# Attention followed by a mixture of experts: eight splits, two bias loads and the last adds moved between engines

## What is computed

```python
x = x + attention(layernorm(x), ctx)      # 4x1024 rows of 256, 16 heads of 64, 64 keys of 192
x = x + ffn(layernorm(x))

def ffn(x):                                # E = 8 experts, top 2, H = 352
    scores = softmax(x @ gate_w.T)
    idx = top_k(scores + gate_b, 2)
    h  = silu((x @ w1[e] + b1[e]) * (x @ w3[e] + b3[e]))     # for the two experts e of a row
    y  = sum over the two of scores[e] * (h @ w2[e] + b2[e])
    z  = the same form with the shared weights sw1, sw3, sw2 (every row)
    return y + z
```

## Time and profile before

| | |
|---|---|
| time, median of three runs | 722.57 us (722.37 to 724.9) |
| the profiled execution | 728.77 us, its span 727.0 us, mean granted clock 0.974 |
| busy: TensorE, VectorE, ScalarE, GpSimd | 92%, 74%, 55%, 59% of the span |
| attention's pipeline | about 95 to 335 us |
| units' phase | 339 to 725 us |

### The profile page before, as it was taken

One profiled execution on the slowest core, in us unless ns is written; L12 is line 12 of the kernel. 1 busy time (PEld: TensorE's weight loads), 2 busy tenths in 40 slices (PEclk: granted clock), 3 DMA queues, 4 the chain that ended last, 5 costly groups with the idle time before them and its releaser, 6 DMA issues.

```text
span 727.0 us, 16811 instructions
## 1 busy us (share of the span) xinstructions
PE 671.5 (92%) x4606; PEld 627.8 (86%) x4607; DVE 537.7 (74%) x1106; ACT 400.9 (55%) x1308; POOL 429.1 (59%) x514
## 2 busy tenths in 40 slices
PE   7997789999999989985699999999999999999976
PEld 6785679998888879874699999999999999999975
DVE  5964788888978878766989866666666666666796
ACT  4984677877767666664564444444444444444432
POOL 4552565454468677665346337677777777775291
PEclk8998999999999999996999999999999999999999
DMA  8201223336526875754851335554444444455694
GB/s 247 78 15 65 66 73 94 104 110 193 161 80 116 187 138 130 111 133 90 154 85 44 79 49 75 75 74 72 72 73 72 72 72 72 72 102 97 150 407 187
DMA packets 77045, 79.03 MB, mean 109 GB/s; under 512 B 21738, under 2 KB 70228, under 8 KB 76980
## 3 DMA queue, kind: packets, MB, share of 16 engines
q1 hardware_dynamic: 56932, 53.66, 29.3%
q0 software_dynamic: 15760, 18.96, 16.2%
q10 hardware_dynamic: 4288, 5.64, 2.4%
HBM read 47.22 MB, written 31.01 MB: 108 GB/s over the span
## 4 chain that ended last, share of the span: by engine, by line
PE 32%; issue 22%; POOL 13%; DMA 11%; SPq 9%; DVE 7%; ACT 5%; POOLq 0%; ACTq 0%; DVEq 0%
PE ps L1269 26%; DMA slots_scratch<-record,slot 8%; POOL xrow L718 6%; SPq L542 5%; SPq L543 4%; PE ps L1376 3%; POOL acc_scratch L725 2%; POOL slots_scratch L668 2%; DMA xin<-in_x 1%; PE ps L1360 1%; ACT prob L791 1%; DVE AU L1121 1%; DMA wk_raw<-in_L_xattn_Wk 1%; PE ps L1345 1%; ACT AU L803 1%
## 5 line engine op out<-in xcount | busy, mean ns | idle before, releaser
L725 POOL DMA_INDIRECT acc_scratch<-yrow,slots x71 | 112.7, 1587 | 70.2 <-ACT yrow L920 56.3
L920 ACT ACTIVATE yrow<-ps,slots 128x256 f32<-128x256 f32 x71 | 33.7, 474 | 147.7 <-PE ps L1269 147.7
L1269 PE MATMUL ps<-AU,pTh 128*128 128x256 f32 x512 | 101.3, 290 | 0.0
L1195 DVE TENSOR_TENSOR uv<-ps,b 128x704 f32<-128x704 f32 x71 | 63.3, 892 | 47.8 <-PE ps L1269 47.8
L1269 PE MATMUL ps<-w13h,uxTh 128*128 x284 | 97.8, 344 | 0.0
L1269 PE MATMUL ps<-AU,xTh 128*128 128x512 f32 x256 | 97.4, 425 | 0.0
L668 POOL DMA_INDIRECT slots_scratch<-record,slot x64 | 66.1, 1033 | 45.8 <-DMA slots_scratch<-record,slot 33.6
L1269 PE MATMUL ps<-w13h,uxTl 128*128 x284 | 91.6, 322 | 0.0
L1269 PE MATMUL ps<-w13l,uxTh 128*128 x284 | 91.3, 322 | 0.0
L718 POOL DMA_INDIRECT xrow<-xn_scratch,slots x71 | 69.8, 983 | 27.2 <-issue 19.8
L791 ACT ACTIVATE prob<-ps,nmax 128x64 f32<-128x64 f32 x256 | 76.3, 337 | 14.4 <-DVE nmax L1048 14.3
(11 more groups left out here) (241 smaller groups left out, 2000.9 us busy)
## 6 DMA issues: line engine op xcount, KB each, us to landing
sums<-acc_scratch SPq DMA_DIRECT2D x16, 512.0 KB, 11.3
w_raw<-in_L_ffn_w SPq DMA_DIRECT2D x16, 352.0 KB, 4.1
xin<-in_x SPq DMA_DIRECT2D x32, 128.0 KB, 2.5
xres<-in_x SPq DMA_DIRECT2D x32, 128.0 KB, 3.0
acc_scratch<-x SPq DMA_DIRECT2D x32, 128.0 KB, 2.3
xn_scratch<-xn SPq DMA_DIRECT2D x32, 128.0 KB, 2.6
xn2T_scratch<-xn2T SPq DMA_DIRECT2D x32, 128.0 KB, 3.7
xrow<-xn2T_scratch SPq DMA_DIRECT2D x32, 128.0 KB, 5.0
```

The source lines that it names most:

```text
L725: pool.indirect_dma_start(acc_dram[u % 2], bass.IndirectOffsetOnAxis(ap=slots[:, u, 0:1], axis=0), yrow[:, m % YRING, :], None, compute_op ...
L920: act.activation(yrow[:, y, :], ps[:, 6 + m % 2, 0:D], ACT.Copy, scale=slots[:, bass.ds(u, 1), 1].bitcast(F32)).then_inc(y_ok, 1)
L1195: dve.tensor_tensor(uv[:, :, :], ps[:, 1 + 2 * p:3 + 2 * p, 0:H], bias, ALU.add).then_inc(bias_ok, 1)
L1269: last = pe.matmul(out, stationary(k, a), moving(k, b), start=(k == 0 and i == 0), stop=(k == n - 1 and i == len(PARTS) - 1 and not more))
```

## The change

- The splits of the experts' first weights: `high13` of experts 0 to 4 at ScalarE's attention steps 30 to 34, `low13` of experts 0 to 4 at VectorE's attention steps 33 to 37; the remaining three low parts at steps 13 to 15 of the units' phase.
- The biases: a table [128, 2, 8, 352] is loaded with 2 transfers of 128 x 2816 values.
- Behind the routed units (t >= `R1`) ScalarE also copies the rows to PSUM, and VectorE's uxTl subtraction reads that copy; ScalarE waits for `uxTl_ok` of the last routed unit first.
- Quads 5, 6 and 7 are added by VectorE itself at steps 100, 101 and 102; the zrow adds of quads 5 and 6 stand at steps 101 and 103; VectorE no longer waits for GpSimd's adds.

```diff
-        b13 = sb("b13", [P, E, 2 * H], F32)
+        b13 = sb("b13", [P, 2, E, H], F32)
...
-            for e in range(E):
-                for i, b in enumerate((b1, b3)):
-                    sp.dma_start(b13[:, e, i * H:(i + 1) * H],
-                                 b[e, :].rearrange("(a h) -> a h", a=1).to_broadcast([P, H])).then_inc(b13_in, 16)
+            for i, b in enumerate((b1, b3)):
+                sp.dma_start(b13[:, i, :, :].rearrange("p e h -> p (e h)"),
+                             b.rearrange("(a e) h -> a (e h)", a=1).to_broadcast([P, E * H])).then_inc(b13_in, 16)
...
-            for q in range(NT // QUAD):
+            for q in range(NA // QUAD):
                 both = [sums[:, i, q, :, :].rearrange("p a d -> p (a d)") for i in range(2)]
                 pool.wait_ge(sums_in[q], 32)
                 pool.tensor_tensor(both[0], both[0], both[1], ALU.add).then_inc(both_ok, 1)
...
-                if 33 <= s < 33 + EARLY13:
-                    high13(s - 33)
+                if 30 <= s < 30 + EARLY13:
+                    high13(s - 30)
...
-                    act.activation(uxTh[:, p, :], xT, ACT.Copy).then_inc(uxTh_ok, 1)
+                    if isinstance(t, int) and t >= R1:
+                        act.wait_ge(uxTl_ok, R1)
+                        act.activation(uxTh[:, p, :], xT, ACT.Copy)
+                        act.activation(ps[:, 0, p * D:(p + 1) * D], xT, ACT.Copy).then_inc(uxTh_ok, 1)
+                    else:
+                        act.activation(uxTh[:, p, :], xT, ACT.Copy).then_inc(uxTh_ok, 1)
...
-                if s >= 35:
-                    low13(s - 35)
+                if 33 <= s < 33 + EARLY13:
+                    low13(s - 33)
...
-                    dve.wait_ge(both_ok, NT // QUAD)
...
-                    xT = ps[:, 0, 0:D] if is_routed(t, routed) else xrow[:, m, :]
+                    if is_routed(t, routed):
+                        xT = ps[:, 0, 0:D]
+                    elif t >= R1:
+                        xT = ps[:, 0, p * D:(p + 1) * D]
+                    else:
+                        xT = xrow[:, m, :]
...
-                if isinstance(s, int) and 5 + E <= s < 5 + E + E - 3:
-                    low13(s - 5 - E + 3)
-                q = s - NALL + NT // QUAD - 2 if isinstance(s, int) else -1
-                if NA // QUAD <= q < NT // QUAD - 1:
-                    z0 = (q - NA // QUAD) * QUAD
-                    row = sums[:, 0, q, :, :].rearrange("p a d -> p (a d)")
-                    dve.wait_ge(both_ok, q + 1)
+                if isinstance(s, int) and 5 + E <= s < 5 + E + E - EARLY13:
+                    low13(s - 5 - E + EARLY13)
+                if isinstance(s, int) and NALL - 3 <= s < NALL:
+                    q = s - NALL + NT // QUAD
+                    both = [sums[:, i, q, :, :].rearrange("p a d -> p (a d)") for i in range(2)]
+                    dve.wait_ge(sums_in[q], 32)
+                    link(dve.tensor_tensor(both[0], both[0], both[1], ALU.add))
+                if isinstance(s, int) and s in (NALL - 2, NALL):
+                    z0 = (s - NALL + 2) // 2 * QUAD
+                    row = sums[:, 0, (NA + z0) // QUAD, :, :].rearrange("p a d -> p (a d)")
                     dve.wait_ge(z_row_ok, z0 + QUAD)
```

More of the change, by code:

```diff
@@ L1188, in unit_step @@
                         if isinstance(t, int) and t == R0:
-                            dve.wait_ge(b13_in, 32 * E)
-                        bias = b13[:, bass.ds(e, 1), :].rearrange("p e (a h) -> p (e a) h", a=2)
+                            dve.wait_ge(b13_in, 32)
+                        bias = b13[:, :, bass.ds(e, 1), :].rearrange("p a e h -> p a (e h)")
                     else:
```

## The result

The changed kernel takes 729.86 us (median of 20 runs, 726.9 to 737.26). The kernel before, over its own 20 runs, takes 725.19 (722.37 to 729.03); its first three, from which the prediction started, gave 722.57. The ratio is 1.0066 [1.0048, 1.0084]: **4.8 us slower** (the medians are 4.7 apart), where +3.0 was forecast. The sign was right; the time lies 0.9 us above the range. Of the 4.3 us between 725.6 and 729.86, 2.6 are the starting figure, which three runs gave too low, and 1.7 are the change.

What follows compares the result with a forecast made beforehand. TensorE was taken as the bound, losing time in attention's last steps, the units' steps 13 to 17 and the tail. Attention +5.8, units -0.9, tail -1.9 gave +3.0 us: 725.6 us from 722.57, range 718.9 to 729.

Steps and rivals of the forecast that it cites:

- the clock: Attention's end: TensorE's clock falls in the pause ahead of ranks, the product behind mostly at half clock; +2.0 us (0 to +2.9).
- the copy: Behind the routed units: ScalarE's extra copy to PSUM is hidden, 0; without cover 4 us at most.
- the tail: Behind the routed units: fewer hold-ups of VectorE, partly eaten by its own three adds; -1.9 us (+1 to -5).
- ScalarE's three slots: Attention steps 30 to 32: high-part splits delay xn2T by +0.4, +0.95 and +1.35, in sum 2.7 us (0.4 to 4.1).
- The split of step 33: Attention step 33: VectorE's low part lies in its idle time; 0, without that cover 0.8 us.
- The split of step 34: Attention step 34: VectorE's low part directly ahead of the logits' copy delays ranks; +1.6 us (1.2 to 1.7).
- The units' phase: Routed units, steps 16 and 17: two splits fewer; -0.9 us (0 to -1.7).
- The sign that was to prove it wrong: Start of the units' phase, uxTl of tile 0 (before at 338.9), less than 2 us later.
- Rival 1: Attention's end: the clock holds, everything else as forecast without the 2.0; 723.6 us, chance 0.26.
- Rival 2: Drain's whole price: product wholly at half clock, step 33's split uncovered, tail gives only 0.9; +5.7, 728.3 us, chance 0.18.
- Rival 3: Whole tail comes back: step 99's product slips between GpSimd's adds, steps at 3.33 us; -5 there, 720.5 or 718, chance 0.17.
- Rival 4: Tail: lock by start order, VectorE's quads could hold up GpSimd's; no cost, or +1.5 with a late landing (727.1); chance 0.05.

Runs made afterwards that it cites:

- experiment 4: The changed kernel plus 20 unused identity transposes on TensorE in step 35, ahead of the wait for the ranks; 1.0023 of the kernel before.
- experiment 9: The kernel before with only the high parts moved to ScalarE's steps 30 to 34, low parts as before; 1.006 of the kernel before.
- a1: The kernel before with the new places of all the splits alone, high and low parts; 1.0056 of the kernel before.
- a3: The changed kernel without the split in step 34: VectorE's low parts at steps 33, 35, 36, 37, four in the units' phase; 1.0051 of the kernel before.
- b1: The changed kernel itself measured again, on another chip; 1.0067 of the kernel before.
- a4: The kernel of experiment 4: the changed kernel plus 20 unused transposes ahead of the wait for the ranks; 1.0023 of the kernel before.
- c3: The kernel of experiment 9: the kernel before with only ScalarE's high parts moved early; 1.006 of the kernel before.
- b2: The kernel before with only the biases loaded in two transfers; 0.9989 of the kernel before.
- b3: The kernel before with only VectorE's three quads: no PSUM copy, old bias loads and splits; 1.0018 of the kernel before.
- Experiments 7 and 8: 7: b3, and b4 with five copies (1.0018, 0.9995). 8: c4, the kernel before with 12 copies, GpSimd adding all quads (1.0002).
- a2: The changed kernel with the splits back at their places of before; 0.9955 of the kernel before.
- b4: The changed kernel with the splits of before and the PSUM copy in five steps instead of twelve; 0.9995 of the kernel before.
- c1: b4 plus unused transposes in the pauses of attention's steps 34 to 37 and ahead of the first unit; 0.9942 of the kernel before.
- c4: The kernel before with ScalarE's 12 PSUM copies and VectorE's subtraction from PSUM, GpSimd adding all eight quads; 1.0002 of the kernel before.

## Why the prediction missed

**The number.** The range went from -3.7 to +6.4 us around the starting figure of 722.57. As a difference the measured +4.7 lies inside it; the time lies outside because the starting figure, the median of three runs, was 2.6 us below that of twenty. That is luck of the draw and no fault of the mechanism. The mechanism had three terms wrong, and they partly offset each other: the first too small (the clock), the second put at nothing (the copy), the third too small a gain, which the clock can take back (the tail).

**Right.** The mechanism of the drain in every term but the clock. ScalarE's three slots: +0.4, +0.95, +1.35 predicted; +0.38, +1.11, +1.41 in experiment 4, +2.64 in sum in experiment 9. The split of step 33: 0 predicted, 0.3 by experiment 9. The split of step 34: 1.6, measured 1.61. Step 36: -0.5, measured -0.46 or -0.47 in each. The units' phase: -0.9; steps 16 and 17 take 3.33 us in after, where before had some 3.77 each, and from the logits to the last routed bias add it is -0.98 in this pair of profiles. The biases: 0. In the tail: uxTl never held, the product of step 99 held once, quads 5 to 7 without a wait for a landing. The sign that was to prove it wrong, a first uxTl of the units less than 2 us later, came near: 341.43 against 338.86, since after was 5.27 us ahead when the drain began.

**The step that failed first is the clock, a term of the right kind but too small.** I counted one fall, behind the 2.0 to 2.9 us pause ahead of `ranks`, at +2.0. There the loss was 2.4 (5.34 less the 2.99 of before). The same sum had a wait of 2.3 us ahead of the logits' matmuls in step 33, written down as a length only; TensorE lost its clock behind that one too: 1.52 instead of experiment 4's 0.93 for the transposes and 3.85 instead of 2.88 for the product, +1.6. Together +4.0, against 2.0. The bound of this term, +2.9, was too low because it held one product, not because the price of one was unknown. That the clock is the cause of what exceeds the splits' own price is shown by the windows at 0.50 and by experiment 4, where the same splits cost 3.76 in an execution whose clock held, in step 35 with the transposes, in step 33 without them. Rival 1 (the clock holds) didn't happen in any profile with the new splits in which nothing was added. But the forecast and this account share a weakness, that a pause decides: behind the same 2.4 us in step 33 the clock fell in four profiles (after, a1, a3, b1) and held in two (a4, c3), and around tile 31's product in step 35 it fell with pauses of only 0.5 to 1.1 us ahead of `ranks` as well (b2, b3, c3, a3), costing 1.2 to 1.5. What else decides stays open. By the Trainium skill (TensorE: Matmul & The Clock Gate, Why this matters for your kernels) both pauses are short enough to be spared; the trace disagrees.

**The second is the copy, taken as hidden: 0, measured +1.2.** The cover was misread. I counted VectorE's 0.25 us of idle time ahead of uxTl in the earlier trace rows as room for the copy, but the same row says that this idle time ended with ScalarE's uxTh, and the copy stands directly behind uxTh on ScalarE. Time in which VectorE waits for ScalarE is no cover for more work on ScalarE; it grows by it, to 0.91 us in the row above. The copy holds hTh back by the same 0.3 us, and in steps 91 to 94 ScalarE still scales a routed result (0.47 us, L919) ahead of it all. Experiments 7 and 8 pin the price: 21.07 to 21.11 us with the copy, 19.87 to 19.89 without. Into PSUM the copy took 0.38 us, uxTh into SBUF 0.41, so the destination was no mistake; the copy's place in the chain was.

**The third is the end of the tail.** Relieved of the hold-ups VectorE and TensorE came to their last steps as forecast: from uxTl of step 98 to the last row before took 31.28 us, a2, a4 and b4 28.3 to 28.7, a gain of 2.6 to 3.0 (1.9 had been forecast, for the whole tail). In the profiled execution of after, 2.07 us went to the clock in the last two products. With quads on VectorE TensorE pauses for 1.99 or 2.00 us ahead of the last but one Y, in all eight such profiles without transposes there; the clock fell behind that pause in three (after, a3, c1) and held in five (a2, a4, b1, b3, b4). With the quads on GpSimd the pause is 1.62 to 1.66 us, and the clock fell in none of the five (before, a1, b2, c3, c4). So part of the tail's gain is at risk, and the prediction had no term for it.

**What the sum says of the whole.** By the traces after should be 7.84 - 0.98 - 0.8 (b1's tail) = 6.1 us slower, with the clock's fall at the end 7.9. The runs say 4.8, between 3.5 and 6.1. Part of the gap has a trace. Of the six profiles with the splits of before and no transposes, two (b3 and b2) lost the clock ahead of tile 31's product by themselves (6.74 and 6.84 us from tile 30 to 31, instead of 5.46), and so does before in some executions, I assume; and the fall in step 33 came in four of six, not always. Both would bring the typical price under the 6.1 of these traces. But experiment 9 lies the other way, 4.4 by the time and 3.1 by the drain, so these counts explain the gap only in part. TensorE's wait for the first gather doesn't explain the gap: it was 2.65 us in c4 and 4.30 in b3, with a short drain, but also 3.63 in b1 and 3.67 in a3, with a longer one, and nothing in before, after, a2 and c3. So whether a part of the longer drain is covered there stays open.

Rival 2, the whole price, stood nearest with +5.7, though two of its three additions were not what happened: the split of step 33 was covered, and no landing was awaited. Rival 3 failed at its first step, as the product of step 99 was held. Rival 4 cost nothing. The rule of rival 4 (the Trainium skill, SBUF — State Buffer, Who interferes with whom) is borne out in the half that counts here: the product held 2.44 us by an add of GpSimd's that started first, the subtraction that reads one PSUM input at 0.43 beside the same adds.

## What to carry to other kernels

A wait that an edit adds on TensorE's path has two prices: its length, and the half clock of what follows; list every new pause of a few microseconds, small matmuls between them included, and price the burst behind each, as a chance and not as a certainty. An instruction put on a "half idle" engine is hidden only if nobody waits for it or for the one behind it in the queue: read what ended the consumer's idle time before counting it as cover, and do so in each step where the instruction is put, not only in the steps that the edit is for. Where pauses can't be avoided, unused transposes are a cheap try: with them and five copies in place of twelve, without the moved splits, this kernel came 0.6% below the one before.

## What the runs showed of the hardware

- In after the clock fell at 311.2, 0.8 us after a pause of 2.40 us had ended, and came back at 314.6; in a1 and b1 it fell 0.1 and 0.2 us after the same pause, in a3 1.4. Ahead of `ranks` it fell within the pause (324.8, in 322.8 to 325.5). The same pause of 2.40 us in experiment 4 (313.4 to 315.8) left it at full. So the length of a pause alone doesn't decide here.
- Twenty transposes in the pause ahead of `ranks` (2.72 us in after), which left 0.48 us of it idle, kept the clock in experiment 4.
- In several profiles on the other chips an engine of the units' phase stood still for several us near steps 20 and 21, for a releaser that the trace doesn't name; ScalarE in a2_no_splits:

```profile
413.06 0.38 ACT L924 ACTIVATE yrow<-ps 128x256 f32<-128x256 f32 x1 [6.68 <-remote]
```

It comes at the first gathered rows, in kernels with and without the change, and is one reason for the spread of single executions; its cause stays open. From the logits to the last routed bias add the profiles on those chips took 337.8 to 343.5 us, on the first 334.8 and 335.8.
